# The second dense part moved into the program of the mixing and the second attention

## What is computed

```
x = layernorm(x + attention0(x))   # 16 heads of 8 channels, relative positions by clipped tables
x = layernorm(x + mixing(x))       # token shift, sigmoid gate, squared relu
x = layernorm(x + attention1(x))   # 16 heads, sinusoidal relative positions, biases u and v
x = layernorm(x + ffn(x))          # below
```

```
h = silu(x @ w1 * s1) * (x @ w2 * s2)
h = gelu(h @ h1 * s_h1)
h = gelu(h @ h2 * s_h2)
out = h @ w3 * s3
```

## Time and profile before

| | |
|---|---|
| runs | 2020.65, 2015.1, 2013.89 us (median 2015.1) |
| the profiled execution: its time | 2019.39 us |
| its span, first to last instruction | 2017.6 us |
| PE busy | 1726.7 us (86%) |
| ACT busy | 1474.8 us (73%) |
| DVE busy | 1447.8 us (72%) |
| mean granted TensorE clock | 0.948 |

### The profile page before, as it was taken

The page is one execution under the profiler, slowest core; times in us unless marked ns, Lnnn a source line. Parts: engine busy times, 40 slices in busy tenths (PEclk is TensorE's granted clock), DMA queues, the critical chain, the costliest instruction groups (busy, mean ns, idle before and its releaser), DMA issues. The chain is left out here.

```text
span 2017.6 us, 44338 instructions
## 1 busy us (share of the span) xinstructions
PE 1726.7 (86%) x11694; PEld 1041.8 (52%) x11694; DVE 1447.8 (72%) x3492; ACT 1474.8 (73%) x2605; POOL 79.6 (4%) x102
## 2 busy tenths in 40 slices
PE   5379999999999999935766999999999975999998
PEld 2145555555555555524544556655666542455444
DVE  6468888888888888825978888888888853234322
ACT  4458888888888888834877999999999971223222
POOL 0000000000000000002530000000000000000000
PEclk8679999999999999987878999999999997999999
DMA  6778888888888888816899777777777733001100
GB/s 210 267 241 264 266 265 266 262 266 262 264 266 271 266 264 264 242 45 182 297 338 306 214 211 209 216 212 212 211 212 213 212 96 110 21 21 30 32 6 11
DMA packets 414650, 404.59 MB, mean 201 GB/s; under 512 B 37001, under 2 KB 334849, under 8 KB 414465
## 3 DMA queue, kind: packets, MB, share of 16 engines
q1 hardware_dynamic: 414593, 403.93, 66.2%
HBM read 227.02 MB, written 176.30 MB: 200 GB/s over the span
## 5 line engine op out<-in xcount | busy, mean ns | idle before, releaser
L949 ACT ACTIVATE arena<-bank,a_negmax 128x512 f32<-128x512 f32 x1024 | 739.4, 722 | 34.6 <-DVE a_negmax L898 33.6
L898 DVE TENSOR_REDUCE a_negmax<-bank 128x1 f32<-128x512 f32 x1024 | 699.8, 683 | 0.2 <-issue 0.2
L813 PE MATMUL bank<-ident,arena 128*128 128x128 f32 x4096 | 644.3, 280 | 58.4 <-ACT arena L956 50.4
L956 ACT COPY arena<-bank 128x512 f32<-128x512 f32 x1024 | 620.1, 606 | 90.2 <-PE bank L813 77.8
L813 PEld LDWEIGHTS bank<-ident,arena 128*128 128x128 f32 x4096 | 449.7, 141 | 176.4 <-issue 71.4
L890 DVE TENSOR_TENSOR bank<-bank,a_band 128x128 f32<-128x128 f32 (+3 forms) x1024 | 350.0, 342 | 77.2 <-PE bank L794 69.5
L792 PE MATMUL bank<-a_stks 74*128 74x192 bf16 (+7 forms) x1024 | 323.7, 316 | 26.2 <-ACT arena L949 23.5
L826 PE MATMUL bank<-arena,a_vs 128*32 128x512 f32 x2048 | 272.4, 606 | 14.9 <-ACT arena L956 14.9
L792 PEld LDWEIGHTS bank<-a_stks 74*128 74x128 bf16 (+1 forms) x1024 | 100.1, 98 | 250.8 <-ACT arena L949 206.5
L878 DVE COPY_PREDICATED bank<-a_mask,bank 128x128 f32<-128x128 uint32 (+1 forms) x512 | 139.5, 272 | 114.3 <-PE bank L798 112.3
L794 PE MATMUL bank<-a_stks 74*128 74x320 bf16 (+5 forms) x768 | 200.5, 261 | 0.0
(11 more groups left out here) (178 smaller groups left out, 1631.1 us busy)
## 6 DMA issues: line engine op xcount, KB each, us to landing
a_band<-shear_b SPq DMA_DIRECT2D x128, 512.0 KB, 4.9
shear_a<-a_keyside SPq DMA_DIRECT2D x128, 256.0 KB, 3.8
a_sheared<-shear_a SPq DMA_DIRECT2D x128, 256.0 KB, 3.8
shear_b<-a_corr SPq DMA_DIRECT2D x128, 256.0 KB, 2.8
shear_e<-a_corr SPq DMA_DIRECT2D x128, 256.0 KB, 2.2
a_band<-shear_e SPq DMA_DIRECT2D x128, 256.0 KB, 3.1
a_stks<-stack SPq DMA_DIRECT2D x256, 96.0 KB, 3.1
a_stks<-stack SPq DMA_DIRECT2D x384, 48.0 KB, 2.6
```

Of the source, the lines that this page charges most:

```text
L813: last = pe.transpose(turned_bank[k][:, n * 128:(n + 1) * 128], prob[h.slot % 2][:, n, k * 128:(k + 1) * 128], ident[:, :])
L898: v.tensor_reduce(negmax[h.slot % 2][:, n:n + 1], score[:, :], AX.X, ALU.max, negate=True).then_inc(maxed, 1)
L949: nc.scalar.activation(prob[h.slot % 2][:, n, :], score[:, :], ACT.Exp, bias=negmax[h.slot % 2][:, n:n + 1]).then_inc(exped, 1)
L956: nc.scalar.copy(probt[h.slot][:, k, :], turned_bank[k][:, :]).then_inc(copied, 1)
```

## The change

1. **Two phases instead of three.** `dense_phase` becomes `dense(att)`, and its program is written behind that of attention1 in the same block. The stop between attention1 and the dense part goes, with its 109 clears. The 36 semaphores of the dense part are now raised in the `start_phase` of phase 2, which so has 145.
2. **The front of batch 0 moves into the last twelve steps of attention1**, in pieces that `att.program` calls behind each step:

```diff
+            def sync_tail(sp, left):
+                if left == 11:
+                    att.group_landed(sp, H // GROUP)
+                    load_constants(sp, loads[:N_FIRST], c_in)
+                    load_batch(sp, 0)
+                if left == 7:
+                    load_constants(sp, loads[N_FIRST:], late_in)
+            def tensor_tail(pe, left):
+                if left == 4:
+                    pe.wait_ge(c_in, BASE + 16 * N_FIRST)
+                    att.corrected(pe)
+                    out_product(pe, 0)
+                if left == 0:
+                    flip(pe, 0, out_bank)
+            def scalar_tail(act, left):
+                if left == 0:
+                    turn(act, 0, out_bank)
+            def vector_tail(v, left):
+                if 6 <= left <= 9:
+                    invert(v, 0, 128 * (9 - left), 128)
+                if left == 5:
+                    v.wait_ge(c_in, BASE + 16 * N_FIRST)
+                    normalise(v, 0)
+                if left == 3:
+                    residual1(v, 0)
+                if left == 1:
+                    rows(v, 0, pre1, x1n, 1)
+                if left == 0:
+                    keep_rows1(v, 0)
```

3. **What PE waits for between attention1 and the ffn**:

```diff
+            def finished(pe):
+                pe.wait_ge(copied, BASE + NT * NHEAD)
+                pe.wait_ge(exped, BASE + NT * NHEAD)
+                pe.wait_ge(out_copied, BASE + NG)
...
+                    pe.wait_ge(late_in, BASE + 16 * (len(loads) - N_FIRST))
+                    att.finished(pe)
+                    steps(pe, step)
```

4. **SBUF by hand.** Until now each phase allocated its tiles anew. Three regions of every partition take their place, and the tiles of all stages are put in them one behind the other, at multiples of 64 bytes; stages that don't live at the same time overlap:

```diff
+WORK, HEADS, EDGES = (18432, 100352), (100352, 170240), (170240, 229312)
...
+                tile = nc.alloc_sbuf_tensor_at(f"{self.prefix}_{name}", shape, dt, offset=self.at)
+                self.at += size
...
-            prob, probt = [tiles[:, i] for i in range(2)], [tiles[:, 2 + i] for i in range(unroll)]
+            prob = work.pair("prob", [128, NT, T])
+            probt = [work.take(f"probt{i}", [128, NT, T]) for i in range(unroll)]
```

More of the change, by code:

```diff
@@ L489, in opening, with attention @@
             return stage
-        def attention(layer, ctx, kept):
+        def attention(layer):
             rel = layer == 0
@@ L498, in attention @@
             vslots = unroll // GROUP
-            def sb(name, shape, dt=F32):
-                return ctx.enter_context(nc.sbuf_tensor(f"a{layer}_{name}", shape, dt))
+            sb, work = Region(f"a{layer}", HEADS).take, Region(f"a{layer}", WORK)
             def s(name):
                 return sem(f"a{layer}_{name}")
-            arena, ident = kept
             if rel:
@@ L867, in _ @@
                         tensor_step(pe, loops, FIRST + j, last - 1 - j)
+                        after.tensor_tail(pe, last - 1 - j)
                     for k in range(NT):
@@ L941, in _ @@
                         vector_step(loops, FIRST + j, last - 1 - j)
+                        after.vector_tail(v, last - 1 - j)
                 def exp_tile(act, h, n):
@@ L1005, in attention, with mixing @@
             return stage
[L1007 to L1013, removed]
+        def mixing(att):
+            edge, work = Region("m", EDGES), Region("m", WORK)
+            early = Region("m", HEADS, HEADS[1] - HEADS[0] - 16384)
+            sb, pair = edge.take, edge.pair
             def s(name):
                 return sem(f"m_{name}")
[L1018 to L1025, removed]
             wo, bo = sb("wo", [C, C]), sb("bo", [128, C])
@@ new lines, in build, with sync_tail, tensor_tail, scalar_tail @@
+        class Nothing:
+            def sync_tail(self, sp, left):
+                pass
+            def tensor_tail(self, pe, left):
+                pass
+            def scalar_tail(self, act, left):
+                pass
+            def vector_tail(self, v, left):
+                pass
+        att = attention(0)
+        first = opening(att)
+        start_phase()
+        with nc.Block() as block:
+            first.program(block)
+            att.program(block, first, Nothing())
+        end_phase()
@@ L1863, in _tables @@
+        att = attention(1)
+        mix, end = mixing(att), dense(att)
+        start_phase()
+        with nc.Block() as block:
+            mix.program(block)
+            att.program(block, mix, end)
+            end.program(block)
 def _tables(np):
```

543 lines of the change are left out of this document (262 added, 281 removed).

## The result

The changed kernel takes **1992.8 us** (median of four runs, 1991.2 to 1993.3), the kernel before 2017.1 beside it; the ratio is 0.988, its interval 0.9865 to 0.9892. A second set of four gave 1992.9 beside 2014.5 and 0.9886 [0.9869, 0.9902]. Forecast were 1991 and 1983 to 2000. The profiled execution of the changed kernel has a time of 1991.2 and a span of 1989.1 us.

A forecast was written before the change was run, and what follows sets the result against it. ACT was taken to pace the second attention and PE the dense part, with a 31.88 us stretch between. The terms sum to -24.3 us: 1995 from the profiled 2019.4, 1991 as a median; range 1983 to 2000.

The forecast's parts named there:

- Stop and front off PE's path: Between attention1 and the ffn: PE waits only for the last group's copy, 31.88 us become 0.2; -31.7 us.
- The clock: First gated products: PE starts them at once, so they take 6.87 us instead of 9.32; -2.4 us.
- The semaphores: Stop between phases 1 and 2: 36 increments move there at 0.064 us each, unhidden; +2.3 us.
- DVE behind step 9: Attention1's tail: DVE waits 1.6 to 3.0 us for the sums, then does the reciprocal; +2.9 us reach ACT.
- Steps 8 to 6: DVE's insertions behind these steps: 0.9 us each, less 0.2 us of lead over ACT, three times; +2.1 us.
- Step 5: DVE's insertion behind this step: one product and four sums, 1.50 us, less 0.2 us of lead; +1.3 us.
- The weights: ffn weights loaded behind step 7: the band's delay runs beside DVE's insertions; 0 us, between 0 and +9.
- The layout: Placement of buffers throughout the kernel: same shapes and same instructions, so 0 us.
- The third rival: Tiles of both attentions: the placement slows them, 2052 us at 60 ns per exponential and copy pair; chance 0.04.
- the second: Attention1's last steps: the weights hold up the bands, head 2's landing 7 to 9 us late; 1999 us, chance 0.15.
- The first, hidden insertions: Attention1's last steps: insertions fall into DVE's waits, only some 0.5 of 7.9 us remain; 1983 us, chance 0.2.
- the fourth: End of attention1: batch 0's front isn't ready, 10 to 25 us of the gap return; 2001 to 2016 us, chance 0.04.

The follow-up runs named there:

- front_late: The changed kernel with each insertion of batch 0's front on DVE and PE one step later: 1991.9 us, ratio 0.9885 to the kernel before.
- shared_sems: The changed kernel with semaphore clears and increments at launch and at the stop divided over five engines: 1984.2 us, ratio 0.9846 to the kernel before.
- best: The changed kernel with semaphore operations divided over five engines and the ffn's weights loaded behind step 4: 1976.6 us, ratio 0.9803 to the kernel before.
- front_behind: The changed kernel with DVE, PE and ACT doing batch 0's front behind step 0, loads unmoved: 1997.3 us, ratio 0.9911 to the kernel before.

## Why the prediction was right

The time and the range were right, but **two of its terms were wrong and cancelled in part**; that the time came within 2 us is luck. By its own steps:

- *Stop and front off PE's path, -31.7*: -31.5 (31.88 to 0.34). *The clock, -2.4*: -2.2.
- *The semaphores, +2.3*: +2.1, and the price by itself is 0.059 us, not 0.064.
- *DVE behind step 9, +2.9*: ACT waited 3.27 and 0.60 us. The wait for the sums (2.62) is where and as long as forecast (0.9 to 2.6 in the eight traces that have it). But its cause was told too narrowly: front_late took it away and won nothing. Batch 0's loads, as a block on SP's queue, delay the next band as well (landing 7.2 us).
- *Steps 8 to 6, +2.1*: 0.53, 0.52 and 0.26, so +1.3; the lead of 0.2 us was too small. *Step 5, +1.3*: 0.84. *Step 3, +1.2*: 1.10.
- *PE's product, +0.4*: not separable in the trace.
- *The weights, 0, between 0 and +9*: **the step that failed.** Moving them won 6.5 us in the medians (7.6 between shared_sems and best, which are of two sets). In the traces the tail is 72.6 us with them behind step 7 (mean of 73.6, 72.8, 73.9, 70.3) and 66.5 behind step 4 (mean of 67.0, 65.4, 67.5, 66.3): 6.1, of which 5.0 lie between the last group copy but two and the last but one, where the late band is. The forecast let the band land 11.1 to 12.1 us after the weights' first issue (1624.9 to 1636 or 1637) and be needed after 11.4 (1636.3). In the trace the weights go out from 1622.73. DVE is ready at 1633.08 (1632.40 + 0.68), after 10.4: the insertions put the need off by 2.1 (front_behind, without any, has 8.2) and not by 2.7. The band lands after 15.0, in the other five traces with the weights there after 14.0 to 15.1. This was the larger error. The read itself went out when SP had issued the weights (until 1628.88); DVE's edge copy, for which the write ahead of it waits, had ended at 1626.26, so DVE did not hold it. And the sum had the weights' 2.84 MB alone, at 369 GB/s; by the row above some 4.3 MB passed at 285 GB/s in those 15.0 us, an estimate. The Trainium skill, "DMA: Bandwidth & Descriptors", "Queues, rings and completion order", has descriptors taken in ring order on each DMA engine; the landing of 8.0 us behind the weights, against 4.5 at most before, agrees with it, but would also come of a shared rate.
- *Batch 1, 0*: 0. *The layout, 0*: about **-4**. The other wrong term, on the other side. The third rival had looked at the tiles of the steps, which indeed did not move (the exponential has a median of 712 ns, 713 before), and the forecast then gave the layout nothing anywhere but the 0.4 us of the identity matrix; the opening and the mixing were not looked at.

Sum in the tail: insertions and batch 0's loads 6.6 (66.5 less the 59.9 of the three kernels without: 60.3, 59.6, 59.9) where 7.9 were forecast, plus 6.1 for the weights, 12.7 in all. Of the 6.6, the traces do not say how much is insertions and how much batch 0's loads. -31.5 - 2.2 + 2.1 + 12.7 - 4 = -22.9, against -24.2 by the medians of the first set and -21.7 by those of the second.

Of the rivals the second was half true: its mechanism is there, at 6.5 of the 8 us that it gave. The first, hidden insertions, is refuted by ACT's waits and by the 6.6 us, the fourth by the 0.34 us; the third by the attention loop, which kept its length, while the layout acted elsewhere and the other way.

## What to carry to other kernels

Work that is slipped into the last steps of a loop was paid on two accounts here: on the engines, which the trace of before priced well, and on the DMA queue, where a block of loads delays the small transfers that the next steps wait for. Put bulk loads behind the last small one that is waited for, not beside it. Reckon a small transfer's landing from the first issue of the block ahead of it, with all that the queue holds in between and not with the block alone. A wait taken away only counts if the next transfer in that queue is not late too. The semaphore work of a stop is worth dividing over the engines even when the stop can't be removed: 257 operations on one engine were some 15 us.

## What the runs showed of the hardware

- A semaphore increment took SP 0.059 us (by 72 added ones), about 0.08 to 0.09 on the slower of ACT and DVE, 0.14 on the slower of PE and GpSimd; for the clears at the stop the same prices are assumed. Dividing 257 of them over five engines took the stop from 18.4 to 10.4 us.
- Operands at other addresses, with fewer loads of the identity matrix, left the lengths of ACT's and DVE's instructions as they were, but the traces have a shorter opening (3 us) and mixing (4 to 8 us), and the medians are 4.0 us apart.
- Behind loads of 2.84 MB in the same queue a band's read landed 8.0 us after its issue, behind batch 0's loads 7.2 us, where 4.5 was the longest before.
